# Loading the first activations in float32 on the SyncE queue and casting them on ScalarE and VectorE, in a fused attention and feed-forward kernel

## The chip, the cores and the metric

The kernel runs on one Trainium2 chip, on all 8 cores; each core works on one of the 8 sequences of the batch and no core talks to another. The time is the device time of the slowest core in microseconds (us). In the profile, PE is TensorE, PEld its weight loads, DVE is VectorE, ACT is ScalarE, POOL is GpSimd and SP is SyncE.

## The reference, cut to what matters

```
# x: (8, 2048, 1024); 16 heads of 64; one sequence per core
q, k, v = x @ Wq.T + bq, x @ Wk.T + bk, x @ Wv.T + bv
scores  = (q @ k.T) * 64**-0.5 * exp(-alpha * |i - j|)
x1 = layernorm(x + softmax(scores) @ v @ Wo.T + bo)
w_gate, w_up, w_down = fp4 quantize and dequantize, blocks of 16 along the last dim
xq = fp4(x1);  h = silu(xq @ w_gate.T) * (xq @ w_up.T)       # 2816 wide
out = layernorm(x1 + fp4(h) @ w_down.T)
```

All matmuls of the kernel run in bfloat16 with float32 sums; the inputs come from memory in float32.

## The kernel before, in words

The program is a list of operations for each of the five engines. `op(eng, at, fn, waits)` notes one operation with a due time `at`; `finish` sorts each engine's list by `at`, and each engine then works through its list strictly in that order, waiting on the semaphores of the operations named in `waits`. So `at` fixes who stands behind whom; it doesn't set a time. One unit of `at` is a nominal step of the attention.

There are three stages. **First projections** (`at` from -104 to about -2): x arrives transposed, in four quarters of 512 tokens (`xT[:, c]`, c = 0 to 3), with the Q and K weights of head pair 0 (`wqk`) and the first half of the V weights (`wvs`, 512 of 1024 columns). The list `first_jobs` names the projection jobs: a job is 8 matmuls of 512 columns into one of six PSUM banks. Its order is Q0 K0 V0-V3, Q1 K1 V4-V7, K2 V8-V11, K3 V12-V15, Q2, where the digit of Q and K is the quarter and V counts 128-token tiles. Job i is due at -48 + 2i, and its result is copied out of PSUM ("evacuated") just behind it: a V job by one DVE addition (line 433), a K job by one DVE operation (line 440), a Q job by one ACT operation (line 450) and two or three DVE operations (line 457), which prepare Q multiplied with the decay factors. **Attention** (`at` 0 to 512): 32 units (head pair, quarter) of 16 steps; a step is a score matmul (line 470), an exponential on ACT (lines 554 to 570) and the product with V (line 590). Beside it the remaining projections run, and DVE quantizes the feed-forward weights: 60 chunks, each loaded into `wst` (line 726), treated by the seven operations of `quant_chain` (lines 234 to 246), transposed by DMA and stored. `fill_gaps` places those 420 operations into the gaps that a model of DVE's work leaves: it starts at -18, and tries values of `slack` (how late an attention operation may get) from 0.2 upwards until the last one is placed before `at` 498. **Output projection and feed-forward** follow.

All of x, `wqk` and `wvs` is loaded by DMAs issued from POOL, which turn float32 into bfloat16 on the way; they need nothing and stand first in POOL's list, in the order `wqk` of pair 0, x0, `wvs`, x1, x2, x3, `wqk` of pair 1. SP issues three tiny loads (lines 284), and, after waiting for x0, the V bias `bvb` (line 289, 512 KB) and the output bias `bof` twice (line 292, one row each). Four small DVE operations (lines 330 to 335), due at -93.8 to -93.5 and so ahead of all evacuations, split that output bias into two bfloat16 rows in `bo33`.

The memory of the attention's result (`attnT`), of V's second half (`V1`), of the exponentials (`PT`, `SD`) and of the weight quantization (`wst` and its neighbours, `O_QZ`) holds nothing during the first stage.

Of the kernel before, what the change touches and what calls it, by code (L numbers as in the profile page):

```python
# [6 lines left out]
F32 = mybir.dt.float32  # L7
BF16 = mybir.dt.bfloat16
U16 = mybir.dt.uint16
AF = mybir.ActivationFunctionType  # L10
# [4 lines left out]
D = 1024  # L15
NP = 8
NTT = T // 128
NCT = D // 128
QC = 512
# [75 lines left out]
def build_program():  # L95
# [3 lines left out]
    xT_h = dram("xT", [NQC, 128, NCT * QC])  # L99
# [3 lines left out]
    wv_h = dram("wv", [2, 128, NCT * 512])  # L103
# [19 lines left out]
    p = Prog()  # L123
    es = ExitStack()
    with es:
# [62 lines left out]

        ring = [sb(f"ring{i}", D, F32, O_X + 4 * KB * i) for i in range(4)]
# [62 lines left out]
        d_x = sems("dX", 4)  # L252
        d_w = sems("dW", 2)
        d_v = sem("dWV")
        t_x, t_w, t_v = {}, {}, {}

        def load_x(c, a):
            t_x[c] = op(PO, a, lambda e: e.dma_start(
                out=xT[:, c], in_=xT_h[c].rearrange("p (c t) -> p c t", t=QC)),
                sem=d_x[c], k=16)  # L260
# [8 lines left out]
        def load_v(g, a, free):  # L269
            t_v[g] = op(PO, a, lambda e: e.dma_start(  # L270
                out=wvs, in_=wv_h[g].rearrange("p (c m) -> p c m", m=512)),
                [free], sem=d_v, k=16)

        load_qk(0, -104, None)
        load_x(0, -103)
        load_v(0, -102, None)
        load_x(1, -101)
        load_x(2, -100)
        load_x(3, -99)
# [3 lines left out]
        for dst, src in ((bqs, bq_h), (bks, bk_h), (aneg, al_h)):  # L283
            t_c = op(SP, -100, lambda e, dst=dst, src=src: e.dma_start(out=dst, in_=src),
                     sem=d_c, k=16)
        bof = sb("bof", D, F32, O_R2 + 40 * KB)
        boh = sb("boh", D, F32, O_R2 + 44 * KB)
        d_b = sem("dB")
        t_b = op(SP, -96, lambda e: e.dma_start(out=bvb, in_=bv_h), [t_x[0]], sem=d_b, k=16)
        d_o = sem("dO")  # L290
        for r0 in (0, 32):
            t_o = op(SP, -96, lambda e, r0=r0: e.dma_start(
                out=bof[r0:r0 + 1, :], in_=bo_h), [t_x[0]], sem=d_o, k=16)
# [12 lines left out]
        for v in Vt:  # L306
            t_one = op(DV, -95.5, lambda e, v=v: e.memset(
                v.rearrange("p (k d) -> p k d", d=72)[:, :, 64:72], 1.0))
# [20 lines left out]
        b0 = op(DV, -94.0, lambda e: e.memset(bo33[0:64, :], 0.0))  # L329
        b1 = op(DV, -93.8, lambda e: e.tensor_copy(out=bo33[0:1, :], in_=bof[0:1, :]),  # L330
                [b0, t_o])
        b2 = op(DV, -93.7, lambda e: e.tensor_copy(out=bo33[32:33, :], in_=bof[32:33, :]),
                [b1])
        b3 = op(DV, -93.6, lambda e: e.tensor_copy(out=boh[32:33, :], in_=bo33[32:33, :]), [b2])
        t_bo = op(DV, -93.5, lambda e: e.tensor_tensor(
# [70 lines left out]
        def put_proj(job, keys, bi=PB):  # L406
# [3 lines left out]
            if kind == "V":  # L410
                g, tt = a_, b_
                need = [t_x[tt // 4], t_v[g]]
            else:
                hp, c = a_, b_
                need = [t_x[c], t_w[hp]]
            tok = None
            kk = fa + 0.02
            for i in range(NCT):
                kk = max(kk, keys[i])
                if kind == "V":  # L420
                    fn = lambda e, i=i: e.matmul(  # L421
                        out=pt, lhsT=xT[:, tt // 4, i, (tt % 4) * 128:(tt % 4 + 1) * 128],
                        rhs=wvs[:, i, :], start=(i == 0), stop=(i == NCT - 1))
                else:
                    w = wqk[hp % 2][0 if kind == "Q" else 1]
                    fn = lambda e, i=i, w=w: e.matmul(  # L426
                        out=pt, lhsT=w[:, i, :], rhs=xT[:, c, i, :],
                        start=(i == 0), stop=(i == NCT - 1))
                last = i == NCT - 1
                tok = op(TE, kk, fn, ft + need if i == 0 else [], signal=last)  # L430
# [110 lines left out]
        def put_exp(u, j):  # L541
# [34 lines left out]
            need = [f] + [v_tok[(g, k)] for k in st[1:]] + [t_one if u == 0 and first else None]  # L576
# [64 lines left out]
        for i, job in enumerate(first_jobs):  # L641
            put_proj(job, [-48.0 + 2.0 * i] * 8, bi=(4, 5, 0, 1, 2, 3)[i % 6])
# [56 lines left out]
        def fill_gaps(slack):  # L699
            t, i, out, ka = t_of(-18.0), 0, [], -18.0  # L700
# [506 lines left out]
```

How the kernel before makes its waits and increments, by code:

```python
    def emit(self, eng, e):  # L79
        done = {}
        for (_, _, fn, waits, sem, k, _) in self.ops[eng]:
            need = {}
            for t in waits:
                if t.val > need.get(t.sem, (0,))[0]:
                    need[t.sem] = (t.val, t.sem.h)
            for s, (v, h) in need.items():
                if v > done.get(s, 0):
                    e.wait_ge(h, v)
                    done[s] = v
            i = fn(e)
            if sem is not None:
                i.then_inc(sem.h, k)
# [2 lines left out]
def build_program():  # L95
# [1042 lines left out]
        LAG = 1  # L1138
        for tt in range(NTT + LAG):
            if tt < NTT:
                job_g(tt)
                if tt + 2 < NTT:
                    start_x1(tt + 2, pe[0] - 10.0)
            if tt >= LAG:
                job_d(tt - LAG)
        END = pe[0] + 100.0
        for r in sorted(out_last):
            op(SP, END, lambda e, r=r: e.wait_ge(d_rs[r].h, d_rs[r].n), [], signal=False)
        p.finish()
```

## Time and profile before

| | before |
|---|---|
| median of 3 runs | 1366.99 us (1366.61 to 1444.18) |
| profiled execution: its time | 1369.19 us |
| profiled execution: span of the slowest core (core 0) | 1367.6 us |
| spans of the 8 cores | 1347.0 to 1367.6 us |
| PE busy | 1187.2 us, 87% of the span |
| DVE busy | 1054.5 us, 77% |
| ACT busy | 687.9 us, 50% |
| POOL busy | 194.9 us, 14% |
| mean granted TensorE clock, core 0 | 0.956 |

A span is the time from the first to the last instruction of a core. Busy shares are averages over three stages with different limits, and the change touches the first stage. Of that stage the timeline (which instruction stands when, and what its engine waited for) says most.

### The profile page before, as it was taken

How to read it: one execution, taken by the hardware profiler on the slowest of the kernel's cores; microseconds unless marked ns; L12 is line 12 of the kernel's file. 1: busy time of each engine (PE TensorE's matmuls, PEld its weight loads, DVE VectorE, ACT ScalarE, POOL GpSimd, SP SyncE). 2: the span in 40 equal slices, each digit the busy share in tenths (PEclk: the TensorE clock that was granted, in tenths of full speed). 3: DMA queues.
4: the chain of work that ended last, by engine and by line, in shares of the span. 5: the costliest groups of instructions: out<-in, count | busy, mean ns of one | idle time of the engine just before them, and what ended most of it. 6: DMA issues, size and time to landing. Idle time of an engine off the chain costs nothing.

```text
span 1367.6 us, 18907 instructions; the slowest of 8 cores (1347.0 to 1367.6 us)
## 1 busy us (share of the span) xinstructions
PE 1187.2 (87%) x5856; PEld 461.5 (34%) x5856; DVE 1054.5 (77%) x1408; ACT 687.9 (50%) x803; POOL 194.9 (14%) x387
## 2 busy tenths in 40 slices
PE   3888898989888888888887779789999999999993
PEld 1322233323222222222222223244444444444441
DVE  2697888878878888787788448679987888888871
ACT  1076777868777878777778622312122221222212
POOL 2001111111111111111111123300011101111001
PEclk9999999999999999999999899989999999999997
DMA  9564545444354553645545836983333433324321
GB/s 145 108 152 106 123 105 120 121 104 130 81 118 107 111 138 104 140 112 147 139 130 132 216 119 213 325 253 83 86 86 83 115 83 86 86 76 107 83 63 57
DMA packets 179317, 167.33 MB, mean 122 GB/s; under 512 B 141842, under 2 KB 141842, under 8 KB 178324
## 3 DMA queue, kind: packets, MB, share of 16 engines
q1 hardware_dynamic: 164132, 127.97, 35.9%
q0 software_dynamic: 15088, 38.16, 11.8%
q8 instruction: 50, 0.82, 0.3%
q14 instruction: 47, 0.39, 0.1%
HBM read 111.30 MB, written 34.34 MB: 106 GB/s over the span
## 4 chain that ended last, share of the span: by engine, by line
PE 41%; DVE 26%; issue 13%; DMA 12%; ACT 4%; POOL 2%; DVEq 1%; POOLq 0%; ACTq 0%; SPq 0%
PE ps L1033 14%; PE ps L590 9%; PE ps L1102 6%; PE ps L470 5%; PE ps L426 4%; DVE AV L613 3%; DMA den_scr<-AV 3%; DMA cD<-den_scr 3%; PE ps L421 2%; DMA recD<-rec_scr 2%; DMA rec_scr<-cR 2%; DVE fr L234 2%; DVE attnT L636 2%; DVE SD L521 2%; DVE wst L239 2%
## 5 line engine op out<-in xcount | busy, mean ns | idle before, releaser
L562 ACT ACTIVATE PT<-ps,tab 128x1024 bf16<-128x1024 f32 x384 | 407.0, 1121 | 132.5 <-PE ps L470 130.7
L590 PE MATMUL ps<-PT,V 128*128 128x512 bf16 (+1 forms) x1280 | 318.6, 354 | 63.5 <-DVE AV L613 59.8
L470 PE MATMUL ps<-Q,KT 64*128 64x512 bf16 (+1 forms) x1280 | 210.5, 352 | 41.6 <-DVE SD L521 32.0
L1033 PE MATMUL ps<-wuT,x1qT 128*128 128x512 bf16 (+1 forms) x768 | 169.0, 363 | 10.6 <-DVE hb L1048 10.6
L426 PE MATMUL ps<-xTs,wqk 128*128 128x512 bf16 x512 | 149.7, 402 | 30.4 <-DMA xTs<-xT 17.2
L1033 PE MATMUL ps<-wgT,x1qT 128*128 128x512 bf16 (+1 forms) x768 | 168.0, 362 | 2.3 <-ACT sg L1043 2.1
L590 PEld LDWEIGHTS ps<-PT,V 128*128 128x128 bf16 x1280 | 91.3, 99 | 227.9 <-issue 214.2
L1102 PE MATMUL ps<-wdT,hqT 128*128 128x512 bf16 x704 | 154.6, 379 | 2.7 <-DMA hqT<-hq 2.7
L470 PEld LDWEIGHTS ps<-Q,KT 64*128 64x128 bf16 x1280 | 50.8, 94 | 234.0 <-issue 233.7
L859 ACT ACTIVATE junk<-ring 128x1024 bf16<-128x1024 f32 x16 | 16.9, 1057 | 197.2 <-DVE ring L1110 197.2
L1043 ACT ACTIVATE sg<-ps 128x512 f32<-128x512 f32 (+1 forms) x96 | 51.2, 553 | 127.7 <-PE ps L1033 110.1
L1033 PEld LDWEIGHTS ps<-wuT,x1qT 128*128 128x128 bf16 x768 | 75.4, 98 | 88.5 <-issue 12.0
L1033 PEld LDWEIGHTS ps<-wgT,x1qT 128*128 128x128 bf16 x768 | 74.6, 98 | 83.4 <-issue 7.6
L1048 DVE TENSOR_TENSOR hb<-sg,ps 128x512 f32<-128x512 f32 (+1 forms) x96 | 60.5, 631 | 48.7 <-ACT sg L1043 24.4
L521 DVE TENSOR_TENSOR SD<-ps,tab 128x512 f32<-128x512 f32 x128 | 86.6, 677 | 14.2 <-PE ps L470 13.9
L1102 PEld LDWEIGHTS ps<-wdT,hqT 128*128 128x128 bf16 x704 | 68.8, 98 | 84.4 <-issue 3.1
L570 ACT ACTIVATE PT<-ps,tab 128x512 bf16<-128x512 f32 x128 | 81.1, 686 | 11.1 <-PE ps L470 11.1
L239 DVE SCALAR_TENSOR_TENSOR wst<-wst,qr 128x1024 f32<-128x1024 f32 (+1 forms) x60 | 79.5, 1325 | 3.0
L246 DVE SCALAR_TENSOR_TENSOR wqo<-wqo,qs 128x1024 bf16<-128x1024 bf16 (+1 forms) x60 | 79.6, 1326 | 2.5
L234 DVE TENSOR_REDUCE qr<-wst 128x64 f32<-128x1024 f32 (+1 forms) x60 | 79.1, 1318 | 2.2 <-DVE wqo L246 2.1
L617 POOL DMA_DIRECT2D den_scr<-AV x64 | 31.7, 500 | 338.9 <-DVE AV L613 238.8
L426 PEld LDWEIGHTS ps<-xTs,wqk 128*128 128x128 bf16 x512 | 50.1, 102 | 87.6 <-issue 48.3
(80 smaller groups left out, 1220.8 us busy)
## 6 DMA issues: line engine op xcount, KB each, us to landing
ring<-x_scr SPq DMA_DIRECT2D x32, 512.0 KB, 5.2
wst<-wg SPq DMA_DIRECT2D x22, 512.0 KB, 4.4
wst<-wu SPq DMA_DIRECT2D x22, 512.0 KB, 4.2
wst<-wd SPq DMA_DIRECT2D x16, 704.0 KB, 4.6
recD<-rec_scr POOLq DMA_DIRECT2D x64, 128.0 KB, 3.5
out<-ring POOLq DMA_DIRECT2D x16, 512.0 KB, 6.4
wg_scr<-wtr SPq DMA_DIRECT2D x22, 256.0 KB, 4.4
wu_scr<-wtr SPq DMA_DIRECT2D x22, 256.0 KB, 5.0
```

What stands on the lines that cost most here:

```text
L234: (1.22 * k, lambda e: e.tensor_reduce(out=r, in_=blk(src), axis=AX.X, op=ALU.max, apply_absolute_value=True)),
L239: (1.23 * k, lambda e: e.scalar_tensor_tensor(out=blk(xn), in0=blk(src), scalar=X_MUL, in1=bc(r), op0=ALU.mult, op1=ALU.mult)),
L246: (1.23 * k, lambda e: e.scalar_tensor_tensor(out=blk(o), in0=blk(o), scalar=Q_MUL, in1=bc(s), op0=ALU.mult, op1=ALU.mult)),
L426: fn = lambda e, i=i, w=w: e.matmul(out=pt, lhsT=w[:, i, :], rhs=xT[:, c, i, :], start=(i == 0), stop=(i == NCT - 1))
L470: return op(TE, a, lambda e: e.matmul(out=out, lhsT=KT[hp % 2][r0:r0 + 64, kt * 128:(kt + 1) * 128], rhs=QR[u % 3][n][r0:r0 + 64, q0:q1], ...
L521: f = dv(km, 0.69, lambda e: e.tensor_tensor(out=SD[n][:, 512 * (b % 2):512 * (b % 2) + 512].rearrange("p (h q) -> p h q", h=2), in0=dt.re ...
L562: f = op(AC, k0, lambda e: e.activation(out=PT[ri], in_=src, func=AF.Exp, scale=scl), need)
L570: f = op(AC, k0, lambda e, scl=scl, part=part: e.activation(out=part(PT[ri]), in_=part(src), func=AF.Exp, scale=scl), need if i == 0 else ...
L590: tok = op(TE, ka, lambda e, h=h, k=k, c0=c0, q0=q0, w=w: e.matmul(out=ps_ab[h][:, q0:q0 + w], lhsT=VV[g][:, k, hp % 4, 8 * h:8 * h + 128] ...
L1033: tk = fop(TE, t0, lambda e, i=i, wT=wT, pst=pst: e.matmul(out=pst[g][:, 0:F], lhsT=x1qT[tt % 2][:, i, :], rhs=wT[:, n0:n0 + nn, i, :], st ...
L1048: mu, t = urgent(t0 + 0.05, 0.68 * F / 512, lambda e: e.tensor_tensor(out=hb[hs][:, c0:c0 + F], in0=sg[g][:, 0:F], in1=ps_u[g][:, 0:F], op ...
L1102: tk = fop(TE, t0, lambda e, it=it, c=c: e.matmul(out=ya[:, c * 512:(c + 1) * 512], lhsT=hqT[tt % 2][:, it, :], rhs=wdT[:, 4 * c:4 * c + 4 ...
```

## The change

The four quarters of x and the first `wvs` are no longer cast by the DMA. Each is loaded in float32 by two DMAs from SP (its first and its second half of the contraction rows, h = 0 and 1) into a staging tile in memory that is unused at that time (`xst` 0 to 3, `vst`), and cast by two operations of 1024 columns each: half 0 on ACT, half 1 on DVE. The first and the fifth matmul of a job wait for the cast of half 0 and half 1. The POOL queue keeps the two `wqk` loads. `bvb` and `bof` no longer wait for x0 and stand in the SP queue behind `wvs` and behind x3. The job Q2 moves from the end of `first_jobs` to the head of its quarter. The output bias operations move from -94 to -9.6, the initialisation of V's second half to -10, the first weight chunks are loaded at -20 and wait for the cast of `wvs` in place of x3, and `fill_gaps` starts at -9.

```
+        xst = [sb(f"xst{i}", NCT * QC, F32, o) for i, o in enumerate(
+            (O_AT, O_AT + 16 * KB, O_R2, O_R2 + 30 * KB))]
+        vst = sb("vst", NCT * 512, F32, O_QZ)
+        FIRST_AT = -48.0
...
+        def cast_load(a, ac, src, dst, stage, sm):
+
+            toks = []
+            for h in range(2):
+                lo = slice(HW * h, HW * h + HW)
+                ld = op(SP, a + 0.1 * h, lambda e, lo=lo: e.dma_start(
+                    out=stage[:, lo], in_=src[:, lo]), sem=sm[h], k=16)
+                for i in range(2):
+                    c = slice(HW * h + HW // 2 * i, HW * h + HW // 2 * (i + 1))
+                    if h == 0:
+                        tk = op(AC, ac + 0.01 * i, lambda e, c=c: e.activation(
+                            out=dst[:, c], in_=stage[:, c], func=AF.Identity), [ld])
+                    else:
+                        tk = op(DV, ac + 0.01 * i, lambda e, c=c: e.tensor_copy(
+                            out=dst[:, c], in_=stage[:, c]), [ld])
+                toks.append(tk)
+            return toks
...
         load_qk(0, -104, None)
-        load_x(0, -103)
-        load_v(0, -102, None)
-        load_x(1, -101)
-        load_x(2, -100)
-        load_x(3, -99)
         load_qk(1, -98, None)
...
+        load_x(0, -104, -60.0)
+        t_v[0] = cast_load(-103, -59.0, wv_h[0], wvs.rearrange("p c m -> p (c m)"),
+                           vst, d_v0)
+        bof = sb("bof", D, F32, O_EV)
+        boh = sb("boh", D, F32, O_EV + 4 * KB)
         d_b = sem("dB")
-        t_b = op(SP, -96, lambda e: e.dma_start(out=bvb, in_=bv_h), [t_x[0]], sem=d_b, k=16)
+        t_b = op(SP, -102, lambda e: e.dma_start(out=bvb, in_=bv_h), sem=d_b, k=16)
+        load_x(1, -101, FIRST_AT + 2.0 * 6 - 5.0)
+        load_x(2, -100, FIRST_AT + 2.0 * 12 - 5.0)
+        load_x(3, -99, FIRST_AT + 2.0 * 18 - 5.0)
         d_o = sem("dO")
         for r0 in (0, 32):
-            t_o = op(SP, -96, lambda e, r0=r0: e.dma_start(
-                out=bof[r0:r0 + 1, :], in_=bo_h), [t_x[0]], sem=d_o, k=16)
+            t_o = op(SP, -98, lambda e, r0=r0: e.dma_start(
+                out=bof[r0:r0 + 1, :], in_=bo_h), sem=d_o, k=16)
...
-        b0 = op(DV, -94.0, lambda e: e.memset(bo33[0:64, :], 0.0))
-        b1 = op(DV, -93.8, lambda e: e.tensor_copy(out=bo33[0:1, :], in_=bof[0:1, :]),
+        b0 = op(DV, -9.6, lambda e: e.memset(bo33[0:64, :], 0.0))
+        b1 = op(DV, -9.5, lambda e: e.tensor_copy(out=bo33[0:1, :], in_=bof[0:1, :]),
                 [b0, t_o])
...
         for c in range(NQC):
-            if c < 2:
+            if c < 3:
                 first_jobs.append(("Q", 0, c))
             first_jobs.append(("K", 0, c))
             first_jobs += [("V", 0, t) for t in range(4 * c, 4 * c + 4)]
-        first_jobs.append(("Q", 0, 2))
...
-                tok = op(TE, kk, fn, ft + need if i == 0 else [], signal=last)
+                tok = op(TE, kk, fn, (ft if i == 0 else []) + (list(need[i // 4]) if i % 4 == 0 else []),
+                         signal=last)
...
-            t, i, out, ka = t_of(-18.0), 0, [], -18.0
+            t, i, out, ka = t_of(-9.0), 0, [], -9.0
...
-                          [w_read.get(k - 2), t_x[3] if k < 2 else None],
+                          [w_read.get(k - 2)] + (t_v[0] if k < 2 else []),
                           sem=d_wl[k % 2], k=16)
 
-        w_load(0, -40.0)
-        w_load(1, -39.9)
+        w_load(0, -20.0)
+        w_load(1, -19.9)
```

## Rows read from the trace of the kernel before

**Rows 1.** Timeline, the first 45 us: start us, length us, engine, line, operation, idle before

```profile
1.34 0.91 DVE L307 MEMSET V<- 128x1024 bf16 x1 [1.34 <-PEq L96]
...
14.47 0.96 DVE L318 TENSOR_SCALAR tab<-tab 128x1536 f32<-128x1536 f32 x1 [3.40 <-ACT tab L316]
15.59 0.91 DVE L329 MEMSET bo<- 64x1024 bf16 x1 [0.15 <-issue]
...
17.21 6.22 PE L426 MATMUL ps<-xTs,wqk 128*128 128x512 bf16 x16 [17.21 <-DMA xTs<-xT]
...
24.41 7.07 PE L421 MATMUL ps<-wvs,xTs 128*128 128x512 bf16 x32 [0.98 <-DMA wvs<-wv]
32.51 0.68 DVE L330 CAST bo<-bof 1x1024 bf16<-1x1024 f32 x1 [16.02 <-DMA bof<-bo_b]
...
34.87 1.22 DVE L335 TENSOR_TENSOR bo<-bof,boh 1x1024 bf16<-1x1024 f32 x1
...
38.64 5.75 PE L426 MATMUL ps<-xTs,wqk 128*128 128x512 bf16 x16 [7.16 <-DVE Q L457]
```

**Rows 2.** Windows of 10 us: busy us of each engine, granted clock, DMA share, GB/s

```profile
10.00:20.00 10.00, 2.79 (x7) 1.02 (x8) 2.95 (x3) 3.20 (x2) 0.00 (x0) 1.00 1.01 160
20.00:30.00 10.00, 9.02 (x36) 3.63 (x35) 0.00 (x0) 0.69 (x1) 0.00 (x0) 1.00 1.00 190
30.00:40.00 10.00, 2.84 (x11) 1.05 (x10) 7.04 (x10) 0.00 (x0) 0.00 (x0) 0.81 1.01 165
```

**Rows 3.** DMA issues of the first 6.4 us: name, KB each, us from issue to landing

```profile
wvs<-wv POOLq DMA_DIRECT2D x1, 1024.0 KB, 21.0
...
wqk<-wk POOLq DMA_DIRECT2D x1, 256.0 KB, 41.8
```

**Rows 4.** The loads of x, by tile, in the first 50 us

```profile
L258 POOL DMA_DIRECT2D xTs<-xT x4: 547/572/587, 2.8 to 4.8; - x4
...
DMA to landing us min/median/max: 14.2/30.5/40.2
```

**Rows 5.** Windows of a later stage in which SP's queue loads without a cast

```profile
870.00:880.00 10.00, 9.78 (x46) 4.22 (x44) 8.61 (x17) 3.41 (x3) 4.39 (x7) 1.00 1.00 352
...
890.00:900.00 10.00, 6.79 (x27) 3.12 (x28) 4.55 (x7) 1.09 (x2) 0.00 (x0) 0.68 0.99 347
```

**Rows 6.** The page's costliest groups: an ACT operation of 1024 columns

```profile
L859 ACT ACTIVATE junk<-ring 128x1024 bf16<-128x1024 f32 x16 | 16.9, 1057 | 197.2 <-DVE ring L1110 197.2
```

**Rows 7.** Timeline, the last jobs and the first scores

```profile
68.40 1.89 PE L426 MATMUL ps<-xTs,wqk 128*128 128x512 bf16 x8
...
70.22 0.69 PE L470 MATMUL ps<-Q,KT 64*128 64x256 bf16 x4
...
73.81 0.61 PE L470 MATMUL ps<-Q,KT 64*128 64x512 bf16 x2 [2.89 <-DVE Q L457]
...
74.35 1.46 PE L426 MATMUL ps<-xTs,wqk 128*128 128x512 bf16 x3
...
76.05 0.68 DVE L521 TENSOR_TENSOR SD<-ps,tab 128x512 f32<-128x512 f32 x1
```

**Rows 8.** Timeline, the first weight chunk on DVE between V evacuations

```profile
58.92 1.21 DVE L234 TENSOR_REDUCE qr<-wst 128x64 f32<-128x1024 f32 x1
...
61.00 0.63 DVE L433 TENSOR_TENSOR V<-ps,bvb 128x512 bf16<-128x512 f32 x1
...
61.54 1.21 DVE L239 SCALAR_TENSOR_TENSOR wst<-wst,qr 128x1024 f32<-128x1024 f32 x1
62.67 0.75 DVE L440 TENSOR_SCALAR KT<-ps,bks 128x512 bf16<-128x512 f32 x1
63.33 0.68 DVE L242 TENSOR_SCALAR wqo<-wst 128x1024 uint16<-128x1024 uint16 x1
...
64.46 0.68 DVE L433 TENSOR_TENSOR V<-ps,bvb 128x512 bf16<-128x512 f32 x1
```

**Rows 9.** Waits of PE from 110 to 700 us: total us, times, longest

```profile
PE ps L590 <- DVE AV L613: 50.5, 24, 3.8
```

**Rows 10.** Timeline of DVE at the end of the attention

```profile
757.64 0.69 DVE L238 RECIPROCAL qr<-qs 128x88 f32<-128x88 f32 x1
766.79 0.20 DVE L623 RECIPROCAL cR<-cD 128x8 f32<-128x8 f32 x1 [8.46 <-DMA cD<-den_scr]
```

More of the change, by code:

```diff
@@ L249, in quant_chain, with load_x @@
             ]
-        d_x = sems("dX", 4)
+        d_x = [sems(f"dX{i}", 4) for i in range(2)]
         d_w = sems("dW", 2)
         d_v = sem("dWV")
+        d_v0 = sems("dWVh", 2)
         t_x, t_w, t_v = {}, {}, {}
[L257 to L260, printed above, removed]
+        HW = NCT * QC // 2
+        AC_DV = (AC, DV)
+        def cast_load(a, ac, src, dst, stage, sm):
[14 more added lines that the diff above has]
+            return toks
+        def load_x(c, a, ac):
+            t_x[c] = cast_load(a, ac, xT_h[c], xT[:, c].rearrange("p c t -> p (c t)"),
+                               xst[c], [d_x[h][c] for h in range(2)])
         def load_qk(hp, a, free):
@@ L269, in load_v @@
         def load_v(g, a, free):
-            t_v[g] = op(PO, a, lambda e: e.dma_start(
+            t = op(PO, a, lambda e: e.dma_start(
                 out=wvs, in_=wv_h[g].rearrange("p (c m) -> p c m", m=512)),
                 [free], sem=d_v, k=16)
+            t_v[g] = [t, t]
         load_qk(0, -104, None)
-        load_x(0, -103)
-        load_v(0, -102, None)
-        load_x(1, -101)
-        load_x(2, -100)
-        load_x(3, -99)
         load_qk(1, -98, None)
@@ L283, in build_program @@
         for dst, src in ((bqs, bq_h), (bks, bk_h), (aneg, al_h)):
-            t_c = op(SP, -100, lambda e, dst=dst, src=src: e.dma_start(out=dst, in_=src),
+            t_c = op(SP, -110, lambda e, dst=dst, src=src: e.dma_start(out=dst, in_=src),
                      sem=d_c, k=16)
-        bof = sb("bof", D, F32, O_R2 + 40 * KB)
-        boh = sb("boh", D, F32, O_R2 + 44 * KB)
+        load_x(0, -104, -60.0)
[3 more added lines that the diff above has]
+        boh = sb("boh", D, F32, O_EV + 4 * KB)
         d_b = sem("dB")
-        t_b = op(SP, -96, lambda e: e.dma_start(out=bvb, in_=bv_h), [t_x[0]], sem=d_b, k=16)
+        t_b = op(SP, -102, lambda e: e.dma_start(out=bvb, in_=bv_h), sem=d_b, k=16)
+        load_x(1, -101, FIRST_AT + 2.0 * 6 - 5.0)
+        load_x(2, -100, FIRST_AT + 2.0 * 12 - 5.0)
+        load_x(3, -99, FIRST_AT + 2.0 * 18 - 5.0)
         d_o = sem("dO")
         for r0 in (0, 32):
-            t_o = op(SP, -96, lambda e, r0=r0: e.dma_start(
-                out=bof[r0:r0 + 1, :], in_=bo_h), [t_x[0]], sem=d_o, k=16)
+            t_o = op(SP, -98, lambda e, r0=r0: e.dma_start(
+                out=bof[r0:r0 + 1, :], in_=bo_h), sem=d_o, k=16)
         iota = lambda c0, pat, base, cm: op(
@@ L305, in build_program @@
         t_i = iota((1932, 1944), [[128, 12]], 1, 1)
-        for v in Vt:
-            t_one = op(DV, -95.5, lambda e, v=v: e.memset(
-                v.rearrange("p (k d) -> p k d", d=72)[:, :, 64:72], 1.0))
+        t_one = {}
+        for g, v in enumerate(Vt):
+            t_one[g] = op(DV, (-95.5, -10.0)[g], lambda e, v=v: e.memset(
+                v.rearrange("p (k d) -> p k d", d=72)[:, :, 64:72], 1.0),
+                ([], t_x[2])[g])
         op(DV, -95.5, lambda e: e.memset(one33, 1.0))
@@ L326, in build_program @@
         sclA = tab[:, 1932:1944]
-        b0 = op(DV, -94.0, lambda e: e.memset(bo33[0:64, :], 0.0))
-        b1 = op(DV, -93.8, lambda e: e.tensor_copy(out=bo33[0:1, :], in_=bof[0:1, :]),
+        b0 = op(DV, -9.6, lambda e: e.memset(bo33[0:64, :], 0.0))
+        b1 = op(DV, -9.5, lambda e: e.tensor_copy(out=bo33[0:1, :], in_=bof[0:1, :]),
                 [b0, t_o])
-        b2 = op(DV, -93.7, lambda e: e.tensor_copy(out=bo33[32:33, :], in_=bof[32:33, :]),
+        b2 = op(DV, -9.4, lambda e: e.tensor_copy(out=bo33[32:33, :], in_=bof[32:33, :]),
                 [b1])
-        b3 = op(DV, -93.6, lambda e: e.tensor_copy(out=boh[32:33, :], in_=bo33[32:33, :]), [b2])
-        t_bo = op(DV, -93.5, lambda e: e.tensor_tensor(
+        b3 = op(DV, -9.3, lambda e: e.tensor_copy(out=boh[32:33, :], in_=bo33[32:33, :]), [b2])
+        t_bo = op(DV, -9.2, lambda e: e.tensor_tensor(
             out=bo33[32:33, :], in0=bof[32:33, :], in1=boh[32:33, :], op=ALU.subtract), [b3])
@@ L411, in put_proj @@
                 g, tt = a_, b_
-                need = [t_x[tt // 4], t_v[g]]
+                need = list(zip(t_x[tt // 4], t_v[g]))
             else:
                 hp, c = a_, b_
-                need = [t_x[c], t_w[hp]]
+                need = [(t, t_w[hp]) for t in t_x[c]]
             tok = None
@@ L575, in put_exp @@
             first, last = j == 0, j == 15
-            need = [f] + [v_tok[(g, k)] for k in st[1:]] + [t_one if u == 0 and first else None]
+            need = [f] + [v_tok[(g, k)] for k in st[1:]] + [t_one[g] if first else None]
             ka = max([k0 + (1.5 if first else 0.5), av_at[0] + 0.02]
@@ L641, in build_program @@
         for i, job in enumerate(first_jobs):
-            put_proj(job, [-48.0 + 2.0 * i] * 8, bi=(4, 5, 0, 1, 2, 3)[i % 6])
+            put_proj(job, [FIRST_AT + 2.0 * i] * 8, bi=(4, 5, 0, 1, 2, 3)[i % 6])
         for i in range(2):
```

## The prediction

> **What bounds the kernel now.** I read the timeline of the first 80 us first, then the windows and DMA landings of the same stretch, and last the waits and DVE's timeline of the attention, to see whether a shift of its start survives to the end. The stage that the change touches shows four waits on TensorE, one after the other. It starts at 17.2 us, when x0 lands; it loses about 1 us at 24.4 until the V weights land; it stands still for 7.2 us before 38.6, because DVE, which works in order, waited 16.0 us for the output bias row and so evacuated nothing [rows 1]; and the second score of the attention waits until 73.8, 2.9 us, for the DVE evacuation of Q2, the last job [rows 7]. The 16 matmuls from 17.2 and the 16 from 38.6 also run partly at half clock: 6.2 and 5.75 us, where 32 warm ones take 7.07, less their overlap 6.9 [rows 1]; warm, a job of 8 is 1.73 us and two are 3.45, so a cold start costs 2.3 us. From 38.6 to 70.3 TensorE runs without a break.
>
> The DMA engines are fully busy from 10 to 40 us at 160, 190 and 165 GB/s [rows 2]. Those are written bytes: the group counts a quarter of x as 1024 KB though it is 2 MiB in memory. Read bytes are about twice that (less in the second window, where the V bias is uncast), some 325 GB/s. Where SP's queue loads without a cast, the windows show 352 and 347 GB/s [rows 5]. So bytes read, not bytes written, look like the limit, and removing the cast may speed the loads by 0 to 8%, not slow them by half.
>
> **The change part by part. Landings.** In MiB read, the order before is wqk 1, x0 2, wvs 2, then x and 0.5 of V bias. x0 landed at 2.8 + 14.2 = 17.0, wvs at 3.3 + 21.0 = 24.3, x3 at 4.8 + 40.2 = 45.0, the last wqk at 5.9 + 41.8 = 47.7 [rows 3, 4]. From 24.3 to 45.0 that is 6.5 MiB, 329 GB/s. By the windows' sum the bytes of x0 and of wvs had moved 2 to 3 us before their landings; I keep this as a lag. The new order on SP's queue is x0, wvs, V bias, x1, x2, x3; beside it runs POOL's queue with both pairs of wqk, 2 MiB in place of 1 ahead of wvs. Up to wvs that is 6 MiB, up to x1 8.5, x2 10.5, x3 12.5. At 325 GB/s with the old start (about 5.2 us by the windows) and lag 3 they land at 27.5, 35.6, 42 and 48.5; at 352 GB/s and lag 2 at 25.1, 32.5, 38.5 and 44.4. x0 lands between 17 and 20. I take the middle for each (wvs 26.3, x1 34.0), because nothing shows how two queues share.
>
> The Trainium skill ("DMA: Bandwidth & Descriptors", Specifications) gives about 358 GB/s as one core's share of HBM. [rows 5] agree with 352 and 347. By that figure alone, with no lag, wvs would land at about 23 us and the gain below would be 7 in place of 3 us. The same page (Issuing engines are not separate DMA queues) says that queues of several engines run on the same 16 DMA engines; it speaks against any gain from spreading the loads over two queues.
>
> **Casts.** Each of the five loads gets two ACT operations of 1.06 us [rows 6] and two DVE operations; the nearest row is the cast of one partition by 1024 columns, 0.68 us [rows 1]. I take 1.4 us for a DVE half; were it without that row's speed, it would be 2.4 as two of the 1.2 us operations over 1024 columns [rows 8]. The sums, 10.6 us ACT and 6.8 us DVE, lie where both engines are idle: ACT is busy 0.7 us in 20 to 40 us and DVE 0 in 20 to 30 [rows 2]. On the path stands only the last cast behind each landing, 1.4 us (h = 0 lands about 3 us earlier, so its 2.1 us on ACT are over by then). For x0, ACT and DVE first have to finish the decay table (DVE until 15.4 [rows 1]): cast not before 16.8, so no first matmul much before 17. DVE waits in order for x1 between the evacuations of V1 and V2; behind it are V2 and V3, whose banks are not needed until V6 and V7. That wait costs nothing. The fifth matmul's wait costs nothing but the half it waits for.
>
> **TensorE.** Q0 and K0 from about 19 take 6.2: until 25. V0 to V3 from wvs's cast, 26.3 + 1.4 = 27.7; 6.9 us, and up to 2.3 if the clock falls: until 34.6 to 36.9. x1 is cast at 35.4, and its first half lets up to four matmuls (0.9 us) go ahead of that. Counted from 35.1, between these, the remaining 17 jobs need 29.4 us, with x2 and x3 long there: V15 ends at 64.5. The ends are 60.3 (wvs follows K0 at once at 24.0, then 21 jobs of 1.73) and 67.6 (wvs cast at 28.9, cold start, 38.2 + 29.4). Before, the last matmul ended at 70.3 [rows 7]. The removed bias wait (7.2) and its cold start (2.3) are the larger part of this; the later wvs and x1 take 3 to 4 back.
>
> **The bias chain and V's second half at the end.** This is what comes late next. DVE now has between V12's and V15's evacuation: the zeroing 0.91, the four bias operations 3.6 (32.51 to 36.09) [rows 1], then, as fill_gaps starts at -9, three quantization operations before V13 (58.92 to 61.00, 2.1), one before V14 (1.1) and two before V15 (63.33 to 64.46, 1.1) [rows 8], and the evacuations, four at 0.6 to 0.7. From V12's last matmul: 0.7 + 1.0 + 3.6 + 2.1 + 0.6 + 1.1 + 0.6 + 1.1 + 0.6 = 11.4; V15's last matmul is 5.2 behind V12's, so V15 is evacuated 6.3 us behind the last matmul. V's second half (0.91 [rows 1]) stands ahead of V12 and is hidden in DVE's idle time. The second score uses V15's bank and can start at 64.5 + 6.3 = 70.8. Before it started at 73.8. Moving Q2 forward takes its 3.5 us tail away and this one, nearly twice as long, replaces it. Net **3 us**. The ends 60.3 and 67.6 give 7.2 and -0.1.
>
> **Attention.** fill_gaps works through the same model, and at step 0 the new plan is 3 or 4 of 420 operations behind the old (old: 13 placed below zero; new by hand: 10 by 0.3), 2.4 to 3.6 us of DVE work. Each unit then carries the same work in a slightly shifted mix. The planner of the kernel before, as its program computes it, settles on slack 1.0 and ends at 490.5 where 498 is allowed (0.8 ended at 499.3, just too late). With DVE about 55% free for it at 1.27 us a step, 3.6 us push the end by 5 steps to 495 or 496: still slack 1.0. Those 3.6 us then lie at the end of the attention, where DVE stood idle 8.5 us on one small DMA alone [rows 10]. I cost them at nothing; without that cover they cost 3.6. The reshuffling against the units' waits for the AV copies, 50.5 us in 24 waits [rows 9], I bound by a sixth of them either way, 8 us, and take zero, as nothing gives it a sign. The feed-forward stage is only shifted.
>
> **Sum.** The profiled execution took 1369.2 with a span of 1367.6, and the median of the runs was 1367.0. 1369.2 - 3 = 1366.2 for such an execution; against the median 1367.0 - 3 = **1364**.
>
> **The rivals.**
> *Early data* (15%): the loads reach 352 GB/s without lag, wvs is cast by 24 us and TensorE never stops after its start. For it: rows 5. Against it: the lag of all loads before. 7 us: 1360, with the mix of the attention down to 1356.
> *Late V weights* (12%, slower): SP's float32 loads share the engines evenly with 2 MiB of wqk which nobody needs yet, and wvs lands late. It decides at a cast of wvs later than about 28.7 us, from where V15 ends after 67.5 and the 6.3 us tail reaches 73.8; each further us is a us. Were the loads held at the 287 GB/s seen between x0 and wvs (17.0 to 24.3), wvs lands at 5.2 + 21.9 + 3 = 30.1 and is cast at 31.5: 3 us slower, 1370.
> *Another mix in the attention* (18%, of it 12% slower, 6% faster): the plan ends beyond 498 and slack becomes 1.5, so that AV copies come up to 0.5 us later in 32 units, or the same effect by chance. 8 to 16 us, less the 3 gained: 1372 to 1380; on the other side 1350 to 1356. Against it: the 2 steps of room.
> *It does nothing* (10%): the bias chain and quantization tail are longer than summed, or DVE's backlog after V15 (3.3 us of quantization ahead of the first SD, which stood at 76.05 [rows 7]) hands back what was gained: 1366 to 1368.
> The *forecast* (45%) is 1361 to 1366.
>
> **How the numbers follow.** Under 1354 I leave some 6%, above 1373 some 8 to 10%; the range is 1354 to 1373. 2%, about 27 us, is what a measurement of this kernel can tell from no change; all cases but the far ends of an unforeseen effect lie inside: same 96%, faster 2%, slower 2%.
>
> **What would show it.** Right: no 7 us gap of TensorE near 31 to 38; first matmul at 17 to 20; V0 at 26 to 29 waiting for a cast of wvs; Q1 at 34 to 37; V15's last matmul near 64.5; a TensorE gap of some 5 us before the scores, put down to DVE's V evacuation, with lines 330 to 335 in front of it; second score at 70 to 72; then 3 us kept through to the feed-forward stage. Wrong: a DMA rate of written bytes in 10 to 40 us well below 300 GB/s (the cast was not free of charge for the loads), DVE casts of 1.2 us, a plan whose last quantization operation lies past the end of the old one by over 10 us, or an attention stage whose length differs by more than 8 us.

## The result, and the profile after

The changed kernel takes 1381.7 us (median of 4 runs, 1378.9 to 1383.1), the kernel before 1367.0 (median of 3, 1366.6 to 1367.8); the ratio is 1.0104, 95% interval 1.0083 to 1.0125. It is slower by 1%, where 0.2% faster was forecast; the time lies above the range (1354 to 1373). In some executions the cores of one die show a lower granted clock and take longer (one of the kernel before took 1444 us); the times and ratios here leave these out, which for the cut-load kernel with the old order, below, leaves one execution, of 1347.6 us, and cores 4 to 7 of the profiled one.

Three stretches of the slowest cores add up to the difference. The first and the last AV copy (they end units 0 and 31 of the attention) stand in one row of each kernel, before and then after; the columns are shortest, median and longest duration in ns, then the starts of the first and last of them:

```profile
L613 DVE COPY AV<-ps x64: 678/679/692, 97.7 to 802.3; 128x512 f32<-128x512 f32 x64
```

```profile
L642 DVE COPY AV<-ps x64: 676/682/691, 95.2 to 813.9; 128x512 f32<-128x512 f32 x64
```

Up to the first copy 2.5 us were gained; from the first to the last 704.6 us became 718.7, 14.1 lost; from the last copy to the ends of the spans it was 565.3 (1367.6 - 802.3) and is 567.4 (1381.3 - 813.9), 2.1 lost. The slowest core of before is a slow one in itself: by the median over the 8 cores, from the first to the last unit's copies, the attention took 691 us before and 713 after. All attention lengths below are such medians, each over the cores of one profiled execution.

The head went as forecast. Timeline of the changed kernel (answers to [rows 1, 7]):

```profile
17.40 1.87 PE L454 MATMUL ps<-xTs,wqk 128*128 128x512 bf16 x4 [17.40 <-ACT xTs L275]
19.24 1.30 DVE L278 CAST xTs<-xst 128x1024 bf16<-128x1024 f32 x2 [3.08 <-DMA xst<-xT]
20.68 4.26 PE L454 MATMUL ps<-xTs,wqk 128*128 128x512 bf16 x12 [1.41 <-DVE xTs L278]
...
28.42 6.20 PE L449 MATMUL ps<-wvs,xTs 128*128 128x512 bf16 x28 [0.61 <-DVE wvs L278]
...
36.21 2.75 PE L454 MATMUL ps<-xTs,wqk 128*128 128x512 bf16 x12 [0.73 <-DVE xTs L278]
...
64.08 1.22 DVE L364 TENSOR_TENSOR bo<-bof,boh 1x1024 bf16<-1x1024 f32 x1
...
69.92 0.79 PE L499 MATMUL ps<-Q,KT 64*128 64x512 bf16 x3 [4.85 <-DVE V L462]
...
71.65 0.61 PE L499 MATMUL ps<-Q,KT 64*128 64x512 bf16 x2 [0.94 <-DVE V L462]
```

The reader is to see short waits for casts where the 7.2 us for the bias row stood, and in exchange 4.85 us before the scores, with the bias chain (line 364 is its last operation) ahead of the last V evacuations. The windows of the same stretch (10 to 40 us, answering to [rows 2]) show the loads, now written in float32, at 276 to 344 GB/s:

```profile
10.00:20.00 10.00, 1.87 (x4) 0.44 (x4) 3.52 (x4) 5.20 (x4) 0.00 (x0) 1.00 0.98 276
20.00:30.00 10.00, 6.86 (x24) 2.58 (x25) 3.46 (x6) 2.58 (x3) 0.00 (x0) 1.00 1.01 313
30.00:40.00 10.00, 9.27 (x44) 4.04 (x43) 5.15 (x9) 4.40 (x5) 0.00 (x0) 1.00 1.01 344
```

The loss lies in the attention. Its waits from 98 to 740 us, of the slowest core of the changed kernel and then of the kernel before (answering to [rows 9], which has another window): who waited for what, us in total, times, longest.

```profile
PE ps L619 <- DVE AV L642: 54.0, 26, 5.6
DVE cR L652 <- DMA cD<-den_scr: 41.3, 20, 4.8
DVE attnT L665 <- DMA recD<-rec_scr: 11.9, 3, 4.4
PE ps L454 <- DVE KT L469: 8.8, 9, 2.0
```

```profile
PE ps L590 <- DVE AV L613: 58.4, 27, 3.9
DVE cR L623 <- DMA cD<-den_scr: 26.1, 12, 4.2
DVE attnT L636 <- DMA recD<-rec_scr: 12.3, 6, 2.8
```

DVE's own waits have grown by 15 us (the second row). TensorE pays in two places: its wait for the AV copies, 54 and 58 us on these two cores, is 50 us before and 57 after by the median over the cores and the whole attention, and the last row of the changed kernel, a wait for the evacuation of a K job (line 469), is 8 us by that median and 0 before. All its idle time in the attention is 106 us before and 118 after.

The two DMA rows name a chain that the prediction passed over. At the end of each unit DVE copies the products out of PSUM; POOL sends the softmax denominators to memory and back as `cD` (4 KB, two DMAs in a row), DVE takes their reciprocal `cR`, POOL sends it out and back as `recD`, and DVE multiplies. The reciprocal is due 5.5 steps behind the last product, and everything behind it on DVE, such as a K evacuation, waits with it. One unit of the changed kernel, in time order by engine (DVE, SP, POOL):

```profile
257.79 1.28 DVE L642 COPY AV<-ps 128x512 f32<-128x512 f32 x2
...
262.57 1.22 DVE L251 SCALAR_TENSOR_TENSOR wqo<-wqo,qs 128x1024 bf16<-128x1024 bf16 x1
265.16 0.20 DVE L652 RECIPROCAL cR<-cD 128x8 f32<-128x8 f32 x1 [1.38 <-DMA cD<-den_scr]
...
261.18 0.33 SPq L755 DMA_DIRECT2D wst<-wg  x1
...
262.19 0.58 POOL L649 DMA_DIRECT2D cD<-den_scr  x1 [1.60 <-DMA den_scr<-AV]
```

The 512 KB load of a weight chunk leaves at 261.2, one us ahead of the tiny load of `cD`, and DVE stands 1.4 us at the reciprocal. The changed kernel does this in every unit from 4 to 16 (median over the cores 1.2 to 2.3 us a unit); the kernel before waits there in only two of those 13, 0.7 us at most. The experiments' kernel with the old order shows the same unit so:

```profile
252.52 1.28 DVE L642 COPY AV<-ps 128x512 f32<-128x512 f32 x2
...
260.27 0.69 DVE L247 TENSOR_SCALAR wqo<-wst 128x1024 uint16<-128x1024 uint16 x1 [0.17 <-DVE wst L244]
260.88 0.19 DVE L652 RECIPROCAL cR<-cD 128x8 f32<-128x8 f32 x1
...
261.03 0.33 SPq L758 DMA_DIRECT2D wst<-wu  x1
...
256.95 0.58 POOL L649 DMA_DIRECT2D cD<-den_scr  x1 [1.63 <-DMA den_scr<-AV]
```

There the load leaves behind the reciprocal. It is issued when the fifth operation of a chunk's quantization has read its tile (line 247), so DVE's order fixes its place against the chain. In units 4 to 16 the two orders are locked in two different phases: by the medians over the cores the load leaves 0.7 to 3.1 us behind the copies in the changed kernel and 5.5 to 7.4 us with the old order.

That phase is not the whole of the loss. From before to after, units 0 to 3 grew from 91.5 to 95.9 us, 4 to 16 from 281.3 to 288.7, 17 to 28 from 269.5 to 275.5, and the last two from 49.6 to 54.9 (medians over the cores). DVE's waits on the two ends of the chain grew from 5.5 to 22.9 us in units 4 to 16, where the attention became 7 us longer; in units 17 to 28 they are 23.7 and 24.4 us, and the 6 us lost there have no row of that chain against them.

### The profile page after: what moved, and what is told of

It is laid out like the page before. It is cut to its first block, busy times and chain, and to the rows that moved or that the text cites. A ratio compares the mean times of both kernels' runs of the same rounds, so it can differ in the third digit from the quotient of the medians.

```text
span 1381.3 us, 18940 instructions; the slowest of 8 cores (1372.4 to 1381.3 us)
## 1 busy us (share of the span) xinstructions
PE 1188.9 (86%) x5856; PEld 460.3 (33%) x5856; DVE 1058.3 (77%) x1418; ACT 697.4 (50%) x813; POOL 191.4 (14%) x382
## 4 chain that ended last, share of the span: by engine, by line
DVE 32%; PE 29%; issue 15%; DMA 15%; ACT 4%; POOL 3%; DVEq 1%; SPq 0%; POOLq 0%; ACTq 0%
PE ps L1062 10%; PE ps L619 6%; PE ps L1131 5%; DMA cD<-den_scr 4%; DMA den_scr<-AV 4%; PE ps L499 4%; PE ps L454 3%; DVE qr L239 3%; DVE fr L239 3%; DVE AV L642 3%; DVE wst L244 2%; DVE attnT L665 2%; DMA recD<-rec_scr 2%; DVE hb L244 2%; DMA xst<-xT 2%
## 5 line engine op out<-in xcount | busy, mean ns | idle before, releaser
L454 PEld LDWEIGHTS ps<-xTs,wqk 128*128 128x128 bf16 x512 | 49.1, 102 | 95.4 <-issue 56.8
```

Of the source, the lines that this page charges most:

```text
L454: fn = lambda e, i=i, w=w: e.matmul(out=pt, lhsT=w[:, i, :], rhs=xT[:, c, i, :], start=(i == 0), stop=(i == NCT - 1))
```

## The experiments

Ratios are to the kernel before on the same chip, with 95% intervals; the intervals of the last two kernels and of the one with the old order contain 1. "Chain waits" is DVE's idle time straight before the reciprocal, plus that before the first multiplication by `recD`, summed over units 0 to 28, median over the cores: 25 + 6 = 31 us before, 42 + 10 = 52 after. The attention of the -6 kernel comes from an execution of 1378.3 us, 9 us above the median of that kernel.

| kernel | ratio | interval | attention us | chain waits us |
|---|---|---|---|---|
| changed, first and again | 1.0104, 1.0083 | 1.0083 to 1.0125, 1.005 to 1.0115 | 713, 713 | 52, 49 |
| changed, old order | 1.0004 | 0.9972 to 1.0037 | 697 | 25 + 5 |
| before, filler from -9 | 1.0060 | 1.0035 to 1.0085 | 700 | 32 + 6 |
| changed, filler from -18 | 1.0027 | 0.9999 to 1.0055 | 698 | 38 + 1 |
| changed, filler from -6 | 1.0001 | 0.9968 to 1.0034 | 704 | 31 + 4 |

**Order of quantization.** In the changed kernel the 407 quantization operations due after step 0 get the due times of before:

```
+        durs = [d for d in durs if d[0] > 0] + [
+            (-17.9, 0.69), (-15.9, 0.69), (-13.9, 0.75), (-11.9, 0.69), (-9.9, 0.69),
+            (-7.9, 0.69), (-5.9, 0.69), (-3.85, 0.75), (-3.8, 0.75), (-3.75, 0.75)]
         durs.sort()
...
-            t, i, out, ka = t_of(-9.0), 0, [], -9.0
+            t, i, out, ka = t_of(-18.0), 0, [], -18.0
```

> The changed kernel, with the 407 quantization operations that are due after step 0 put at exactly the due times of the kernel before (the other 13 between -18 and 0, as there). Theory A (the loss of some 21 us in the attention comes from the other order in which DVE takes quantization and attention operations): the attention stage, from the first to the last AV copy, comes back from a median of 712 us over the cores to 690 to 695, and the kernel to 1362 to 1370; the head may give back 2 to 4 us, since more quantization stands ahead of the last V evacuations. Rival B (something else of the change slows the attention, such as the later first weight loads, the DMA queues or the cores being in step with each other): the attention stays at 708 to 715 and the kernel at 1378 to 1384.

Measured: 1369.9, ratio 1.0004, attention 697 (690 to 695 expected). Nothing of the loads, casts and jobs of the first stage is undone, and of the attention's 22 us 16 are gone, with them the loss in time. Theory A holds against rival B. The head gave its gain back (first copies at 97.5 by the median).

The other three change only where the gap filler starts (-9 in the kernel before, -18 and -6 in the changed one).

> The kernel before with one edit of the change alone: the gap filler starts at -9 in place of -18. Loads, casts, jobs are untouched. Theory A: it loses most of what the change lost, 1375 to 1385, with an attention stage of 705 to 715. Rival B: 1364 to 1370, attention 688 to 695; DVE has 5 us less quantization in the head, which then fits into the attention's idle time.

> The changed kernel with the gap filler starting at -18 again, with the new list of jobs, so that the plan resembles the old one but isn't the same. Theory A, if the size of the lag of quantization counts: 1363 to 1372. Theory A, if each plan is a draw of its own: anywhere from 1360 to 1385. Rival B: 1378 to 1384.

> The changed kernel with the gap filler starting at -6 in place of -9: yet less quantization in the head, and about 2 us less DVE work ahead of the last V evacuations, so the second score comes at 69 to 70 in place of 71.7 us. Theory A with lag: 1380 to 1390, worse than the changed kernel. Theory A as a draw: 1360 to 1385. Rival B: 1377 to 1382, the head's 2 us gained.

Measured: 1376.7, 1372.4 and 1369.2. The first loses 0.6% by that one number, less than expected and with 700 us of attention in place of 705 to 715. The third has the least quantization in the head and is no slower than before, so the lag of quantization doesn't explain the loss; each start gives a phase of its own. In the 224 pairs of core and unit (units 1 to 28), a weight load leaves 0 to 4.5 us behind the end of the AV copies in 146 of the changed kernel, 144 with -18, 46 of before with -9, 47 with -6, 32 with the old order and 32 before. The 144 with the smallest end waits (38 + 1) and only 0.3% lost show that the count alone doesn't give the time.

**The changed kernel again.**

> The changed kernel again, unchanged, beside the others on the same chip: 1376 to 1383 by every theory. Below 1372 the difference of 14 us seen first would be one of chips or days.

1381.7 us, attention 713 (ratio 1.0083): the loss came again, beside another set of kernels, so chance or the day is not the cause.

**Loads held back until cD has landed.** A weight load gets the last load of `cD` ahead of it (`t2`) as one more condition; `chains` collects these.

```
+            chains.append(t2)
...
             src, _, F = chunks[k]
+            for t2 in chains:
+                if t2.at - 0.6 <= a <= t2.at:
+                    a = t2.at + 0.001
+            guard = [t2 for t2 in chains if t2.at < a][-1:]
...
-                          [w_read.get(k - 2)] + (t_v[0] if k < 2 else []),
+                          [w_read.get(k - 2)] + (t_v[0] if k < 2 else []) + guard,
```

> The changed kernel, with its quantization order untouched, but every load of a weight chunk also waits on SP until the last small load of softmax denominators (cD) that is due before it has landed, and is ordered behind it. Theory C (the order of quantization costs nothing by itself; it sets when the 512 KB weight loads are issued, and in the changed kernel that is 0.7 to 3.3 us behind the AV copies in units 4 to 17, on top of the chain of small DMAs on whose end DVE then waits): cD lands 5.0 to 5.6 us behind the copies in most units up to 28, DVE's waits on it fall from some 42 us up to unit 29 to 15 to 25, the attention from 712 to 692 to 700 and the kernel to 1360 to 1370. Rival A' (what counts is how much DVE work the order puts between the copies and the reciprocal): DVE's waits fall little and the kernel stays at 1376 to 1384. Rival D (a delayed weight load makes quantization late and DVE waits there): a new wait of DVE on wst, 1375 to 1390.

> The kernel before with the same guard. Its weight loads fall on the small DMAs in units 18, 19, 21, 23 and 25 only, where DVE waited 3 to 5 us each. Theory C: these waits go, 5 to 12 us, 1355 to 1364. Rival A': 1365 to 1370. Rival D: slower than 1370.

> The changed kernel with the gap filler starting at -6 (first unit's copies at 94.0 in place of 95.4 us) and the guard. Theory C: the two gains add, 1350 to 1362, faster than both kernels. Rivals A' and D: 1365 to 1375 as without the guard.

Measured: ratios 1.0068, 1.0027 and 1.0013 (0.9994 to 1.0032), attention 705, 700 and 700. `cD` lands 5.2 to 5.5 us behind the copies as expected, and the wait at the reciprocal falls from 42 to 13, from 25 to 5 and from 31 to 11 us. But the wait at the other end grows from 10 to 27, from 6 to 23 and from 4 to 20. The waits of the guarded changed kernel, 98 to 740 us:

```profile
PE ps L619 <- DVE AV L643: 68.3, 27, 6.7
DVE attnT L667 <- DMA recD<-rec_scr: 25.3, 13, 4.4
DVE cR L654 <- DMA cD<-den_scr: 11.5, 12, 1.7
```

The load now runs over the chain's second half, whose end stands on DVE shortly ahead of the next AV copies, and TensorE's wait for these copies rises from 54 to 68 us (57 to 73 by the median over the cores). The landings came as theory C has them, its times did not: the three kernels took 1379.6, 1375.1 and 1372.2 us, some 10 us above the top of its ranges. Rival A' had the first of them right, but not the wait at the reciprocal, which fell; rival D's wait of DVE for `wst` doesn't appear. The kernel before lost 9 us of attention by the guard, though its chain waits fell from 31 to 29 us, so their sum doesn't give the price. I had not asked what the moved load would hit next.

**The traffic taken away.** 56 of the 60 weight loads bring 8 columns in place of 1024 or 1408, so the kernel quantizes what lies in the tiles; every engine's list is unchanged.

```
+        N = lambda k, F: F if k in (0, 1, 44, 45) else 8
...
-            loads[k] = op(SP, a, lambda e: e.dma_start(out=wst[k % 2][:, 0:F], in_=src),
+            loads[k] = op(SP, a, lambda e: e.dma_start(
+                out=wst[k % 2][:, 0:N(k, F)], in_=src[:, 0:N(k, F)]),
```

> The changed kernel with 56 of the 60 weight chunk loads cut to 8 columns (16 or so of 512 to 704 KB is left, 4 KB each); all engines do the same operations on what lies in the tiles, so the output is not the reference's. Theory C (the 512 KB loads slow the chains of small DMAs on which DVE waits): cD lands 5.0 to 5.6 us behind the copies in units 1 to 28, DVE's waits on the two ends of the chain up to unit 29 fall from 52 us to under 20, the attention from 712 to 680 to 692 us. Theory A' (DVE's order by itself): 705 to 713.

> The same cut of the loads in the changed kernel with the old order of quantization. Theory C: it comes to within 4 us of the cut changed kernel (without the cut they are 12 us apart), both in the attention and in the whole. Theory A': the 12 us stay.

Measured: 1347.9, ratio 0.9868 (0.9808 to 0.9929), for the changed kernel without the traffic. The attention falls from 713 to 678, chain waits from 52 to 18. On cores 4 to 7 the attention takes 677.5 us in both kernels (median; 668 to 682 in the old order, 670 to 684 in the new), where 697 and 713 stand with the loads; the whole took 1347.6 us with the old order, by one execution. As far as these four cores tell, the order costs only through the loads. The loads cost the old order too: without them it is 19 us shorter. How long the tiny loads of `cD` take from issue to landing, from 190 to 480 us, in the changed kernel, with the old order and with the loads cut:

```profile
DMA to landing us min/median/max: 2.0/3.3/4.2
```

```profile
DMA to landing us min/median/max: 1.8/1.9/4.1
```

```profile
DMA to landing us min/median/max: 1.9/1.9/2.3
```

**The bias chain.** The tail that the prediction had priced, tested by loading the bias rows first and doing the chain where DVE is idle:

```
-            t_o = op(SP, -98, lambda e, r0=r0: e.dma_start(
+            t_o = op(SP, -110, lambda e, r0=r0: e.dma_start(
...
-        b0 = op(DV, -9.6, lambda e: e.memset(bo33[0:64, :], 0.0))
+        b0 = op(DV, -60.6, lambda e: e.memset(bo33[0:64, :], 0.0))
```

(and the four behind it at -60.5 to -60.2)

> The changed kernel with the output bias rows loaded first on SP and its five DVE operations put ahead of the x0 casts, where DVE is idle. The tail behind V15's matmuls should fall from some 6.5 to 2 to 3 us, the second score come at 67 to 68.5 us in place of 71.7 and the first unit's copies at 91 to 92 in place of 95.2. The attention's order is unchanged, so 1376 to 1380 in place of 1381.7 if its length is unchanged.

> The same bias edit in the changed kernel with the old order of quantization: first copies at 93 to 94.5 in place of 97.5, attention 690 to 697, the kernel at 1362 to 1368, up to 0.4% below the kernel before. This would be the change as it was meant, with neither its tail nor its new attention order.

Measured: 1372.9 (1.0043, 1.0010 to 1.0075) and 1366.8 (0.9988, 0.9966 to 1.0009). The second score in the new order:

```profile
64.46 0.70 PE L499 MATMUL ps<-Q,KT 64*128 64x256 bf16 x4
66.38 0.39 PE L499 MATMUL ps<-Q,KT 64*128 64x512 bf16 x2 [1.22 <-DVE V L462]
```

It comes 5.3 us earlier than in the changed kernel, and the first copies at 89.7 in place of 95.4 by the median, both earlier than expected; by the ratios the time falls 5 to 8 us, to below the 1376 to 1380 expected. With the old order the first copies come at 92.4 and the whole can't be told from before. With both costs of the change cut, its gain is at most 5 us (the lower end of the interval).

**Reciprocal and multiplications later.** Loads and quantization stay where they are; the list of durations given to the planner is unchanged.

```
-            t3 = dv(ka + 5.5, 0.15, lambda e: e.reciprocal(out=cR, in_=cD), [t2, rec_st[0]])
+            durs.append((ka + 5.5, 0.15))
+            t3 = op(DV, ka + 7.5, lambda e: e.reciprocal(out=cR, in_=cD), [t2, rec_st[0]])
...
-                norm[u] = dv(km + 0.1 * half, 0.68, lambda e, half=half, lo=lo: e.tensor_tensor(
+                durs.append((km + 0.1 * half, 0.68))
+                norm[u] = op(DV, km + 1.5 + 0.1 * half, lambda e, half=half, lo=lo: e.tensor_tensor(
```

> The changed kernel with the same due times of quantization and so the same weight loads at the same place, but DVE's reciprocal of the denominators due 2 steps later, and the two multiplications at the end of the chain 1.5 steps later. Theory C (the loads cost time because DVE, in order, stands at the reciprocal until the slowed chain ends): DVE's waits on the two ends of the chain up to unit 29 fall from 52 us to under 25, the attention from 712 to 692 to 702, the kernel from 1381.7 to 1362 to 1372. Rival E (the loads cost by their traffic elsewhere, DVE's wait at the reciprocal is only where it shows): 1376 to 1384.

> The same later due times in the changed kernel with the old order of quantization and the early bias operations (1367.3 without). Theory C: its waits, 34 us up to unit 29, fall to 10 to 20: 1355 to 1364, faster than both kernels. Rival E: 1364 to 1369.

> The same later due times in the kernel before. Theory C: its waits, 31 us up to unit 29, fall to 10 to 20 and the kernel to 1358 to 1367. Rival E: 1366 to 1372.

> The changed kernel with the early bias operations (1375.4 without) and the later due times. Theory C: as the first of these less the 5 us of the head, 1357 to 1367. Rival E: 1372 to 1378.

Measured: ratios 1.0098, 1.0098, 1.0103 and 1.0097; attention 711, 710, 708 and 711. All four missed what theory C had said, and all four ended alike; the first ended in rival E's range, the other three above it. In the first, 98 to 740 us:

```profile
PE ps L619 <- DVE AV L642: 69.6, 27, 5.9
...
DVE attnT L667 <- DMA recD<-rec_scr: 31.1, 19, 3.7
DVE cR L653 <- DMA cD<-den_scr: 1.5, 3, 0.9
```

The wait at the reciprocal went, and one of 31 us came at the end of the chain, 15.5 steps behind the product and so just ahead of the next AV copies at 16. By its own numbers theory C failed here. What the rows show is that the edit moved the wait and did not take it away. The kernel before lost 1% by it, with only 2 to 3 us more of chain waits in sum than it had, while TensorE's wait for the AV copies rose from 50 to 73 us (median over the cores): what stands on DVE just ahead of the copies matters more than how long DVE waits in sum. Whether it is the wait there or the 1.4 us of the two multiplications themselves, these runs don't part.

**Both waits away.** As above, but the multiplications stand behind the next unit's copies:

```
-                norm[u] = op(DV, km + 1.5 + 0.1 * half, lambda e, half=half, lo=lo: e.tensor_tensor(
+                norm[u] = op(DV, km + (5.5 if u < NU - 1 else 1.5) + 0.1 * half, lambda e, half=half, lo=lo: e.tensor_tensor(
```

> The changed kernel, quantization and weight loads as they were, with the reciprocal 2 steps later as before, and the two multiplications 3.5 steps into the next unit, behind that unit's AV copies in place of just ahead of them; the chain then has more than 15 us and DVE need not wait at its end. Theory C, in the form that is left after the last four runs (a late chain costs where DVE stands at either end of it, and most where that holds back the next AV copies, on which TensorE waits): DVE's waits on both ends fall under 15 us up to unit 29, the attention from 712 to 685 to 698, the kernel to 1354 to 1368. Rival E (the traffic of the loads costs elsewhere): 1376 to 1384, as with the plain later due times.

> The same in the changed kernel with the early bias operations, whose first copies come at 89.7 us in place of 95.2. Theory C: 1348 to 1363, faster than both kernels by more than the interval. Rival E: 1370 to 1378.

Measured: 1328.5 us, ratio **0.9706** (0.9672 to 0.9740), and with the early bias chain 1320.6 us, **0.9651** (0.9623 to 0.9679). The attention takes 655 us in both. The first kernel's waits, 98 to 740 us, and the issue-to-landing time of `cD` as above:

```profile
PE ps L619 <- DVE AV L642: 14.8, 16, 1.8
DVE cR L653 <- DMA cD<-den_scr: 13.3, 4, 7.8
```

```profile
DMA to landing us min/median/max: 2.0/2.5/4.1
```

`cD` is still slowed (2.5 us by the median), and loads and quantization keep their due times (a load leaves within 4.5 us behind the copies in 141 of the 224 pairs), but DVE hardly stands at the chain: chain waits 7 + 0 us, and TensorE's wait for the copies is 15 us where it was 54. The loss of the change is gone with the loads where they were; theory C had said so, and rival E, by its own numbers, missed.

Both kernels came out some 25 us below the range that theory C had given, and the waits on the chain don't explain that. With the loads cut, chain waits are 18 and 11 us and the attention 678; here they are 7 us and it is 655, 23 us less with at most 11 us less of waiting. The edit also takes the two multiplications, 1.4 us of DVE work, out of the last two steps ahead of the AV copies. With the loads cut they still stand there, and TensorE still waits for the copies (changed kernel, loads cut, 98 to 740 us):

```profile
PE ps L619 <- DVE AV L642: 44.5, 28, 3.1
```

By the median over the cores and the whole attention that wait is 49 and 44 us with the loads cut (new and old order) and 15 here. So this edit does two things, it takes the chain's waits away and it takes work from the way of the copies, and the 58 us from 713 to 655 are what both bring. How much is the chain's stays open: the multiplications moved with the loads cut, or with the old order, would tell, and were not run. That leaves the last link of theory C (the slowed chain costs because DVE stands at its ends) supported and not isolated, and it leaves rival E (the traffic costs elsewhere) without a run of its own that excludes it.

The kernel before with these due times wasn't run either, so how much of the 3.5% needs the change at all is open. The first copies come at 94.6 and 89.8 us in place of 97.6, 3 and 8 us of the 39 and 47; if the rest owes nothing to the change, and no run shows that, its own part is 3 us, and 8 with the bias chain moved.

## Why the prediction was wrong, point by point

**Landings and casts: right.** wvs was cast at 28.3 (27.7 said), x1 at 36.1 (35.4), at 1.3 us for a DVE half (1.4); the loads ran at 276 to 344 GB/s (325 to 352 said). From 20 to 40 us the written bytes rose from 190 and 165 to 313 and 344 GB/s while the DMA engines' busy share stayed at 1.00 to 1.01, so written bytes were not the limit, as said. The Trainium skill ("DMA: Bandwidth & Descriptors", Specifications) states about 358 GB/s as one core's share of HBM. The 344 measured lie under it and agree.

**TensorE and the tail: right.** The last V matmul ended at 64.8 (64.5), the second score began at 71.65 (70.8); the head gained 2.2 us (3 said), with the bias chain as what comes late next. The early bias chain confirms that term. The cold start that the sum kept in reserve for V0 (up to 2.3 us) didn't come: 28 matmuls took 6.20 us. What the prediction calls half clock from 17.2 us on stands in the durations alone (here the first 4 matmuls took 1.87 us); the granted clock reads 1.00 from 10 to 30 us in both kernels.

**The plan: right.** Evaluated for the changed kernel, the planner takes slack 1.0 and ends at 494.2 (495 or 496 said by hand), 10 operations being placed by 0.3.

**Attention: the step that failed.** The reshuffling of DVE's operations in the attention, which the sum bounded by 8 us either way, a sixth of TensorE's waits for the AV copies [rows 9], and took as "zero, as nothing gives it a sign", was off by 16 us (697 against 713, changed kernel with old and new order) to 22 us (691 against 713). I took the shift of 3 or 4 DVE operations for a shift of DVE work alone. But a quantization operation also triggers a DMA, and I didn't count the DMAs issued by what moved. The row that shows the danger stood in the prediction: [rows 10], where DVE waits 8.5 us for one small DMA, read as idle time that gives cover, when it was a priced example of the chain's wait. The 18 waits of DVE on `cD` and `recD` before 740 us (38 us, above) weren't priced at all. Nor did repetition enter: quantization and attention are periodic and nearly in step from unit 4 to 16, so one unlucky phase came back in each of 13 units, where the bound took it for chance. What the runs showed in place of that zero is 16 us, which came with the order (old order) and went with the weight loads (loads cut); in the rows 7 us of the loss lie in units 4 to 16, and which waits make up the rest stays open.

**The rivals.** "Another mix in the attention" named the place, with 12% for slower, by slack 1.5, which didn't come, "or the same effect by chance", and at 1372 to 1380 in place of 1382; it had no mechanism for such an effect. Early data and late V weights had their conditions at a cast of wvs by 24 and after 28.7 us, and it came at 28.3, near the late one. "It does nothing" failed at the head, which gained 2.2 us.

## What to carry to other kernels

When operations on an in-order engine are moved, list the DMAs that each one triggers and see which small, latency-bound DMA chain these will run over; a planner that counts only engine time doesn't see it. An operation that waits for such a chain belongs where its engine has more work in front of it than the chain's worst case, not its best, and never just ahead of what the busiest engine waits for. If the same wait returns in each period, add it up over the periods; here 17 us more of waiting in 13 units cost 7 us. Work that isn't needed soon doesn't belong just ahead of such copies either, waits or not.

## What the runs showed of the hardware

A 4 KB load on POOL's queue takes 1.9 us from issue to landing with the weight loads cut and 3.3 us with them in the changed kernel (medians of 190 to 480 us on the slowest core). Over all cores of the changed kernel it takes 3.2 us in units in which a 512 KB load from SP's queue leaves within 4.5 us behind the copies, and 2.0 us in the others. The chain of two such DMAs ends 5.3 to 6.3 us behind the copies in units without a load in the first 4.5 us, and 6.8 to 9.0 us in units with one (medians over units and cores, each of a kernel that loads the weights in full and unguarded). The Trainium skill says that DMAs of different issuing engines run on the same 16 DMA engines and interleave ("DMA: Bandwidth & Descriptors", Issuing engines are not separate DMA queues). That a load from one queue slows one from the other by 1.2 us agrees. The mean granted clock in the attention was 0.944 in the changed kernel, 0.957 before and 0.969 with both waits away (medians over the cores), and TensorE's busy time there 596, 590 and 576 us; so a part of the difference in length stands in TensorE's busy time and not in its waits.
